# An earlier last shift, result loads without the last mask, and a second engine in the final weighted sums of a routed-expert block

## What is computed

```
xn  = layernorm(x)                       # 2048 tokens x 128
out = x + attn(xn) + ffn(xn)

# attn: a chunked state-space branch (z, x, B, C projections, rotary angles, decays, gate, W_out)
# ffn: 16 experts, top 2 of a softmax for each token, weights w that sum to 1
for ei in range(e):
    h = silu(xf @ W1[ei]) * (xf @ W3[ei])
    y = h @ W2[ei]
    y = (y - mu) * rsqrt(var + EPS) * gamma[ei] + beta[ei]
    out = out + combine[:, ei:ei+1] * y
```

## Time and profile before

| | |
|---|---|
| median of 3 runs | 294.63 us (295.16, 292.88, 294.63) |
| profiled execution | 295.18 us, its span 293.4 us |
| outside the span | 1.78 us |
| busy in the span | PE 88%, DVE 79%, PEld 76%, POOL 73%, ACT 44% |
| granted TensorE clock | 0.9 of full speed or more in 36 of 40 slices, 0.7 in two early ones, 0.5 in the last two |
| DMA | 61.55 MB, mean 210 GB/s |

### The profile page before, as it was taken

The page is one execution under the profiler, slowest core; times in us unless marked ns, Lnnn a source line. Parts: engine busy times, 40 slices in busy tenths (PEclk is TensorE's granted clock), DMA queues, the critical chain, the costliest instruction groups (busy, mean ns, idle before and its releaser), DMA issues.

```text
span 293.4 us, 7388 instructions
## 1 busy us (share of the span) xinstructions
PE 258.2 (88%) x2187; PEld 224.1 (76%) x2190; DVE 230.5 (79%) x635; ACT 129.4 (44%) x412; POOL 214.8 (73%) x292
## 2 busy tenths in 40 slices
PE   2999958699999999999999999999999999999400
PEld 0848834588998899689988988998899789889300
DVE  5688997558778959697988889898959787886256
ACT  2766996334445252535344453435352444442000
POOL 8668996828888888787988788787988884647200
PEclk9999999779999999999999999999999999999955
DMA  5621806984778777868978798889669877740094
GB/s 151 215 89 47 322 2 185 311 232 136 234 238 255 244 239 235 273 201 235 289 231 219 239 265 246 237 259 278 203 204 281 252 243 239 243 150 20 26 293 128
DMA packets 68855, 61.55 MB, mean 210 GB/s; under 512 B 6608, under 2 KB 52304, under 8 KB 68816
## 3 DMA queue, kind: packets, MB, share of 16 engines
q1 hardware_dynamic: 66256, 55.83, 62.8%
q0 software_dynamic: 2560, 5.25, 6.4%
HBM read 56.27 MB, written 4.78 MB: 208 GB/s over the span
## 4 chain that ended last, share of the span: by engine, by line
PE 75%; DVE 9%; DMA 4%; issue 4%; POOL 3%; ACT 3%; SPq 1%; POOLq 0%; DVEq 0%
PE bank L857 21%; PE bank L898 10%; PE bank L852 5%; PE bank L801 5%; PE bank L793 4%; PE bank L816 3%; PE bank L894 3%; PE bank L785 3%; PE bank L781 3%; PE bank L825 2%; PE bank L767 2%; PE bank L810 2%; PE bank L772 2%; PE bank L834 2%; DMA decay<-res_dram 2%
## 5 line engine op out<-in xcount | busy, mean ns | idle before, releaser
L857 PE MATMUL bank<-blkT,w_up 128*128 128x128 f32 x512 | 65.7, 282 | 2.1 <-issue 2.0
L857 PEld LDWEIGHTS bank<-blkT,w_up 128*128 128x128 f32 x512 | 61.6, 195 | 5.5 <-issue 5.2
L622 POOL DMA_INDIRECT res_dram<-xrow,sidx x40 | 40.9, 1021 | 17.1 <-DVE xrow L1381 12.6
L574 POOL DMA_INDIRECT blk<-xn_dram,gidx x40 | 45.5, 1139 | 8.7 <-issue 7.6
L1061 ACT ACTIVATE xrow<-bank 128x512 f32<-128x512 f32 x40 | 24.7, 618 | 33.1 <-PE bank L857 17.2
L898 PE MATMUL bank<-w,xrow 128*128 128x128 f32 x256 | 35.5, 283 | 0.3 <-DVE xrow L1368 0.3
L898 PEld LDWEIGHTS bank<-w,xrow 128*128 128x128 f32 x256 | 31.9, 196 | 1.6 <-issue 1.6
L1285 DVE SCALAR_TENSOR_TENSOR kq<-sd,rms,bias_kq 128x512 f32<-128x512 f32 x32 | 23.3, 767 | 11.6 <-POOL rms L589 7.5
L1353 DVE TENSOR_TENSOR xrow<-xrow,bank 128x512 f32<-128x512 f32 x40 | 27.1, 679 | 6.6 <-issue 4.0
L615 POOL TENSOR_TENSOR rstd<-mv,mhalf 128x1 f32<-128x1 f32 x40 | 26.8, 671 | 3.8 <-DVE mv L1365 3.4
L607 POOL TENSOR_TENSOR qs<-kqT,e_row 128x512 f32<-128x512 f32 x16 | 20.5, 1280 | 6.9 <-ACT kqT L1029 6.6
(11 more groups left out here) (240 smaller groups left out, 609.2 us busy)
## 6 DMA issues: line engine op xcount, KB each, us to landing
w_up<-in_L_ffn_W_dram SPq DMA_DIRECT2D x96, 256.0 KB
w<-in_L_ffn_W_dram SPq DMA_DIRECT2D x48, 256.0 KB
e_row<-e_dram SPq DMA_DIRECT2D x16, 256.0 KB
decay<-l_dram SPq DMA_DIRECT2D x4, 512.0 KB, 5.3
gam<-in_L_ffn_gamma_dram SPq DMA_DIRECT2D x32, 64.0 KB
shift_y<-in_L_ffn_beta_dram SPq DMA_DIRECT2D x32, 64.0 KB
decay<-res_dram SPq DMA_DIRECT2D x4, 320.0 KB, 4.3
acc<-in_L_attn_u_dram SPq DMA_DIRECT2D x4, 256.0 KB, 3.6
```

The source lines that it names most:

```text
L574: g.indirect_dma_start(out=blk[:, b % SLOTS, :], out_offset=None, in_=xn_dram, in_offset=bass.IndirectOffsetOnAxis(ap=gidx[:, entry(b):ent ...
L622: g.indirect_dma_start(out=res_dram, in_=res[:, b % HALF, :], in_offset=None, out_offset=bass.IndirectOffsetOnAxis(ap=sidx[:, entry(b):ent ...
L857: last = m(bank[out][:, c * P:(c + 1) * P], w_up[:, u % SETS, n, c * P:(c + 1) * P], blkT[:, b % 2, :], start=True, stop=True)
```

## The change

Four edits, none in iterations 0 to 15:

1. In the last iteration `shift_block(39)` stands in front of `mask(15)`; it stood behind `gate_y(15)`.
2. SP's wait in front of the result loads asks for 8 masks, where it asked for 16.
3. ACT multiplies the second choices' results by their weights, in place (`weigh_results`). DVE adds the first choices as before, tile by tile, and then the weighted second choices of a whole part with one `tensor_tensor`.
4. The parts are 4, 5, 4 and 3 tiles, and were 5, 5, 4 and 2. `add_out(15)` stands in front of the first part and not behind it.

```diff
-        PARTS = (0, 5, 10, 14, NT)
+        PARTS = (0, 4, 9, 13, NT)
...
-                    sp_.wait_ge(s["sd_ready"], NT)
+
+                    sp_.wait_ge(s["sd_ready"], TOPK * T // (NH * P))
...
+            def weigh_results(q):
+
+                act.wait_ge(res_in[q], 16 * TOPK)
+                for t in range(PARTS[q], PARTS[q + 1]):
+                    second = decay[:, :, :].rearrange("p t c -> p (t c)")[:, T + t * DM:T + (t + 1) * DM]
+                    last = a(second, second, ACT.Copy, scale=wtop[:, 1, t:t + 1])
+                last.then_inc(second_ready, 1)
+            for q in range(4):
+                weigh_results(q)
...
                     product(b0)
+                if not first:
+                    shift_block(b1 - 2)
                 if second:
                     mask(t - 1)
...
-                if b1 is not None:
+                if b1 is not None and first:
                     shift_block(b1 - 2)
                     product(b1)
...
-                dve.wait_ge(s["acc_done"], PARTS[q + 1])
+                p0, p1 = PARTS[q], PARTS[q + 1]
+                dve.wait_ge(s["acc_done"], p1)
                 dve.wait_ge(res_in[q], 16 * TOPK)
-                for k in range(TOPK):
-                    for t in range(PARTS[q], PARTS[q + 1]):
-                        last = stt(acc[:, t, :], d[:, k * T + t * DM:k * T + (t + 1) * DM], wtop[:, k, t:t + 1],
-                                   acc[:, t, :], ALU.mult, ALU.add)
-                    if k == 0:
-                        last.then_inc(fin_step, 1)
-                        dve.wait_ge(fin_step, q + 1)
-                last.then_inc(fin_ready, 1)
-            add_results(0)
+                for t in range(p0, p1):
+                    last = stt(acc[:, t, :], d[:, t * DM:(t + 1) * DM], wtop[:, 0, t:t + 1], acc[:, t, :],
+                               ALU.mult, ALU.add)
+                last.then_inc(fin_step, 1)
+                dve.wait_ge(fin_step, q + 1)
+                dve.wait_ge(second_ready, q + 1)
+                both = acc[:, p0:p1, :].rearrange("p t d -> p (t d)")
+                tt(both, both, d[:, T + p0 * DM:T + p1 * DM], ALU.add).then_inc(fin_ready, 1)
             add_out(NT - 1)
-            for q in range(1, NBATCH):
+            for q in range(NBATCH):
                 add_results(q)
```

More of the change, by code:

```diff
@@ L294, in build @@
         res_in = sems("res_in", 4)
-        fin_ready, fin_step, out_done = (sem(n) for n in ("fin_ready", "fin_step", "out_done"))
-        PARTS = (0, 5, 10, 14, NT)
+        second_ready, fin_ready, fin_step, out_done = (sem(n) for n in (
+            "second_ready", "fin_ready", "fin_step", "out_done"))
+        PARTS = (0, 4, 9, 13, NT)
         BY_ACT = (0, 1)
```

## The result

| | before | with the change |
|---|---|---|
| median | 295.16 us (15 runs, 292.64 to 295.85) | 291.6 us (15 runs, 289.83 to 293.13) |
| ratio to before, with 95% interval | | 0.991 (0.9884 to 0.9935) |
| profiled execution, its span | 295.18, 293.4 us | 291.83, 289.8 us |
| start of PE's last up-projection | 265.71 us | 264.78 us |
| from there to the end of the span, the "tail" | 27.7 us | 25.0 us |

The change makes the kernel faster by 0.9% (0.65 to 1.16), on 294.63 us 2.65 us. The prediction was 292.0 us with a gain of 2.67. The medians lie 3.6 us apart, and so do the two profiled spans; the means of the 15 runs on each side are 294.60 and 291.93 us, 2.66 apart, and that is what the ratio says.

What follows compares the result with a forecast made beforehand. Bound at the end by shift, scatter, loads through part two, 22 adds and one store; -1.94 - 0.6 - 0.33 + 0.2 = -2.67 us on the 294.63 us median gave 292.0 us, 8-in-10 range 290.4 to 293.4.

Steps and rivals of the forecast that it cites:

- The frame: Kernel's end as a chain: shift, scatter, loads up to the end of part two, 22 adds, one store.
- The shift, -1.94: Block 39's shift ahead of the last mask lets POOL's last scatter start 1.94 us earlier.
- SP's wait, 0: Asking for 8 masks before the result loads is worth nothing, since the old condition would already be met.
- The parts, -0.6 for the landing and +0.2 for the store: 128 KB less through part two lands it 0.6 us earlier; a last store of 3 tiles costs 0.2 us more.
- The adds, -0.33: From part two on, DVE's adds with ACT's weighing take 5.91 us, where 22 adds took 6.24.
- the sum would be -2.3: If the multiplies stayed on DVE, as the Trainium skill's rule says, the adds' term would be 0, the sum about -2.3.
- The signs: Expected in the changed profile: idle DVE before part two, ACT rows of 0.39 us, wide adds of 0.68, 0.82, 0.55 us.
- the hole: DVE idles about 1.1 us between part one's wide add and the adds of part two.
- Rival A: Result loads land evenly and DVE never idles before part two: gain 3.9 us, time 290.7 us; chance 0.36.
- Rival B: Smaller parts bring nothing, or ACT takes 387 ns each: gain 1.6 to 2.2 us, 292.4 to 293.0 us; chance 0.12.
- C: Rival: something else holds the last scatter, so it doesn't move; 0.7 us of gain left, 293.9 us; chance 0.03.
- D: Rival: ACT's weighing bounds the adds; no gain at 0.66 us each, 298.1 us at 0.95; chance 0.04.

Runs made afterwards that it cites:

- e1: Kernel before with only the last block's shift moved ahead of the last mask: 293.42 us, ratio 0.9936 to before, tail 25.5 us.
- e2: Changed kernel with the shift put back behind the gate: 293.48 us, ratio 0.9956 to before, tail 26.6 us.
- e5: Changed kernel with SP's wait for all 16 masks put back: 289.85 us in one run, tail 24.8 us.
- e4: Changed kernel with the old parts of 5, 5, 4 and 2 tiles: 291.43 us, ratio 0.9887 to before, tail 24.1 us.
- e11: The e4 kernel measured and traced again: 290.37 us, ratio 0.9862 to before, tail 25.0 us.
- e3: Changed kernel without ACT's weighing, DVE adding both choices tile by tile: 291.58 us, ratio 0.9892 to before, tail 26.2 us.
- e10: The changed kernel measured and traced again: 291.75 us, ratio 0.9888 to before, tail 24.9 us.
- e13: Changed kernel with parts 5, 5, 4, 2 and POOL making part two's wide add: 294.07 us, ratio 0.9969 to before, tail 27.5 us.
- e6: Changed kernel with the loads of parts three and four held until part two landed: 293.11 us in one run, tail 26.3 us.
- e9: Changed kernel with the second choices' loads issued by ACT's queue, the first choices' by SP's: 291.14 us, ratio 0.9896 to before, tail 24.9 us.
- e7: Changed kernel with each of ACT's 16 weighings made twice: 295.19 us in one run, tail 26.8 us.

## Why the prediction was right, and where its steps were not

- **The frame held.** Shift, scatter, loads to the end of part two, adds, one store: each link stands in the trace after in this order.
- **The shift, -1.94:** measured -1.94 at the scatter and -1.93 at the first load; e1 and e2 show that it alone does this (in the tail, with load 4's scatter, 2.3 and 1.6). The mask's delay of 0.28 us cost nothing: `add_out(15)` ran at 274.30, four us before the first result.
- **SP's wait, 0:** e2 and e5 agree.
- **The parts, -0.6 for the landing and +0.2 for the store:** in the pair of profiled executions DVE's start on part two moved 0.37 us beyond the shift's 1.93, and over 13 traces 128 KB are 0.45 us, so -0.6 was too much. The store was 0.24 (2.25 us from DVE's last add to the end before, 2.49 after). This gain is about cancelled by the extra tile of work behind part two. The prediction booked that tile under the adds, and so credited the parts with something that no run shows them to bring as a whole (e4, e11).
- **The adds, -0.33:** this was the mis-sized step. Measured: 5.58 us against 6.24, -0.66. The hand-overs were put at 0.1 us each. The wide add in fact starts 0.04 us behind the adds in parts three and four, where ACT is done already, and the overlap at a part's start is 0.08. Split rightly, ACT and the wide adds are worth 1.2 us (e3) of which the extra tile takes back 0.4. The sentence that without them the sum would be -2.3 is therefore wrong: it left the extra tile out. With 24 adds behind part two (6.77 us against 6.24) the links give -1.93 - 0.37 + 0.53 + 0.24 = -1.5, and e3's tail is 1.5 us better than before.
- **Sum:** -1.93 - 0.37 - 0.66 + 0.24 = -2.72, against the prediction's -2.67. The landing was put 0.2 us too high and the adds 0.3 us too low, and the two cancelled. So the closeness of the forecast is partly luck: another landing of load 4 moved the tail of one program by 0.9 us (e4, e11).
- **The signs:** the hole (1.27 against 1.1 us), ACT's 0.39 us and the wide adds (0.69, 0.82 and 0.56 us) came as said; the 5.9 us from part two's first add to the last wide add were 5.58. Of the two signs of being wrong, `add_out(15)` waited for PE, but before any result was there, and part three was waited for by ACT alone, without a cost.
- **Rival A** (no hole, gain 3.0 to 3.9) was seen once, in e4 with five tiles in part one (gain 3.7). In the changed kernel the hole was there in both traces, 1.27 and 0.74 us (e10). The prediction's reading that the slowest share sets the landing is borne out by the last of the 32 steps, 0.66 us behind the 31st in the changed kernel.
- **Rival B:** ACT's price was the cheap one, 389 ns. B's other half, that the parts bring nothing, is near to what e4 and e11 show; the adds made up for it. **C** and **D** did not happen.
- **The rule of the Trainium skill against the edit** ("ScalarE: Activation LUTs", section "Rules for kernel authors", additions and multiplies on VectorE): it sends work by speed per element. In e3, which follows it, DVE was the engine everything waited for and ACT idle, and its tail is 1.2 us longer. By that row the rule doesn't hold where the other engine is idle and VectorE is the bound.
- **The granted clock:** 0.50 in the last slices of before. In the tail it plays no part, since PE has no work there; the engines that do show the same durations in both kernels.

## What to carry to other kernels

Follow the chain at a kernel's end back to the last piece of work that a transfer waits for, and look at what stands in front of it in its engine's order without being needed: one statement moved ahead of a mask and a gate brought 1.9 of the 2.7 us. Where results arrive in parts, count what stands behind each landing, because a smaller first part moves work there, and judge an edit together with the tile it displaces. Trace a kernel twice before a difference of half a us is called an effect: one load's landing moved the end by 0.9 us between two traces of one program. Give spare multiplies to an engine that is idle and doesn't hinder the busy one: ACT was such an engine here, POOL was not.

## What the runs showed of the hardware

- DVE's add of 128 x 128 f32 took 1.68 us instead of 0.34 when POOL ran an add of 128 x 640 on other columns of the same two tiles at the same time: it ended 0.16 us behind POOL's 1.52 us instruction (e13), and DVE's line 1303 takes 0.855 us instead of 0.419 beside POOL's line 566 in the loop. The Trainium skill, "VectorE: DVE Perf Modes", section "Two Vector instructions with no wait between them", names a second SBUF read interface that VectorE shares with GpSimd; both rows agree with an exclusive use of it.
- The landing of the same load scatters by almost a us from one execution to the next (6.8 and 7.8 us behind the first issue in e4 and e11, one program). Most of that is the last of 32 steps of its semaphore, 0.0 us behind the 31st in e4 and 0.7 in e11. Holding the later loads back (e6, 6.7 us) or issuing from two engines (e9, 7.1 us) did not take the late step away.
- ACT's multiply of 128 x 128 f32 by one operand per partition, in place in SBUF, takes 0.389 us and follows its like in 0.293 to 0.295 us (changed kernel, e7).
